# Self attentions of a two-layer latent stack: head halves on row halves, unrolled tiles, masks added by TensorE

## The chip, the cores and the metric

The kernel runs on one core of a Trainium2 chip. The metric is device time in microseconds for one execution. TensorE multiplies matrices from SBUF into PSUM, VectorE, ScalarE and GpSimd work elementwise and in reductions, and SyncE issues the DMAs; all run at once and wait for each other through semaphores. GpSimd doesn't read PSUM here; VectorE and ScalarE do.

## What is computed

A tensor `x` of 16 sequences with 64 tokens of 128 channels passes six residual blocks, each on a layer norm of `x`. Three of them hold a self attention with 16 heads of 8 channels:

```python
x = x + L0_cross_attention(ln(x), ctx)            # 1601 keys per sequence
x = x + L0_attn(ln(x))                            # stage one: causal self attention within a sequence
x = x + L0_experts(ln(x))                         # 8 experts, top 2
x = x + L1_block(ln(x), ctx)                      # cross attention, then self attention (stage two), then ffn
x = x + L1_attn(ln(x))                            # stage three: quantised, attends across the batch
x = x + L1_experts(ln(x))

def L0_attn(x):
    Q, K, V = heads(x @ W_Q), heads(x @ W_K), heads(x @ W_V)
    scores = einsum('bhqd,bhkd->bhqk', Q, K) / D_HEAD ** 0.5 + causal
    return merge(softmax(scores) @ V) @ W_o
```

Stage two has biases and no mask. Stage three has the tensor's first axis (16) as its length and its second (64) as its batch, so a token attends to 16 others; the kernel keeps groups of 64 tokens and masks out the pairs that don't belong together (`block_mask`). Everything is float32.

## The kernel before

The whole program is one pass over hand-written queues: each engine has its own list of instructions, and `at(engine, stage, step)` makes an engine wait for the semaphore of a named step. The stages `"a0"`, `"a1"` and `"a2"` are the self attentions one, two and three.

The 1024 tokens are 8 tiles (`PAIRS`) of 128, two groups of 64 tokens each. All heads of a group are done at once: the keys of a group are spread into a matrix of 128 rows (channels) by 16 x 64 columns (head, key), in which a column holds only the 8 channels of its head and zeros elsewhere. For a tile of two groups that is `kbd`, 128 x 2048. The steps of a tile, by line:

- `keys` (L436): VectorE copies the tile's queries to a buffer of its own (L439) and spreads the keys of the first group (L440, L390); GpSimd spreads those of the second (L398, L390) and waits for the copy of the queries. In its loop GpSimd runs a tiny instruction first (L257).
- `scores` (L327): TensorE multiplies queries by `kbd`, four calls of 128 rows x 64 columns with 512 moving columns; the two groups write to the two halves of the PSUM partitions.
- `subtract_max` (L442): VectorE adds the mask where there is one (L448), takes the maximum of each head (L450) and subtracts it (L451).
- ScalarE takes the exponential (L376) and copies the tile's values into a buffer with sum columns (L379).
- TensorE transposes the probabilities in 8 blocks (L344), ScalarE copies them out of PSUM (L384), TensorE multiplies them by the values (L352), 16 calls of 18 columns.
- `normalise` (L454): VectorE divides by the sums (L460, L464; in stage three one scaling more, L462).

Tiles alternate between two lanes, each with its own PSUM banks (scores in two, transposes and results in two more) and one buffer each for keys, probabilities and values. Each engine walks through rounds of two tiles; rounds 1 and 2 of four are in a loop (`Fori`). The keys of tile t + 2 go into the buffer of tile t, so they wait for the scores of t, and on VectorE they stand behind `subtract_max(t)`:

```python
for lane in range(2):
    subtract_max(i, lane)
    if not (isinstance(i, int) and i == ROUNDS - 1):
        keys(i + 1, lane)
    if lane == 1:
        normalise(i, 0)
    elif not (isinstance(i, int) and i == 0):
        normalise(i - 1, 1)
```

Before the first tile VectorE moves Q and K from PSUM (L406 to L416), writes the sum columns of both lanes (L433), spreads two tiles' keys and masks all values in one instruction (L483), which needs TensorE's value projection (L322) and frees its banks. After the last tile the heads are transposed (L314) and multiplied by the output weights. After its share of stages one and three, GpSimd splits the first experts' weights (L576, L578).

A call of a float32 matmul is two MATMUL instructions in the records; one with operands of type float32r is one instruction. TensorE calls go through a helper, so they show line 262.

## Time and profile before

| | us |
|---|---|
| median of 3 runs (1338.19 to 1339.38) | 1338.86 |
| the profiled execution | 1333.34 |
| its span | 1331.1 |

| engine | busy us | share of the span |
|---|---|---|
| TensorE matmul | 1041.1 | 78% |
| VectorE | 715.7 | 54% |
| ScalarE | 496.4 | 37% |
| GpSimd | 225.6 | 17% |

The mean granted TensorE clock is 0.883 of full speed. A row of the timeline gives start, duration, engine, line, operation, output tile and input tiles, the form (partitions x elements), a count when neighbours are merged (then the duration is from the first's start to the last's end), and in brackets the idle time before it with what ended it. PE is TensorE's matmul, DVE is VectorE, ACT is ScalarE, POOL is GpSimd. PEclk is the granted clock: 1.00 is 2.4 GHz, 0.50 is 1.2 GHz, a value between is a stretch with both. Tiles show under the name of the memory they lie in: `small` the queries of both lanes, `work_area` and `PT` the keys, `ctxT` Q, K and the result, `nat_area` the masked values, `PS` PSUM.

### The profile page before, as it was taken

How to read it: one execution, taken by the hardware profiler on the slowest of the kernel's cores; microseconds unless marked ns; L12 is line 12 of the kernel's file. 1: busy time of each engine (PE TensorE's matmuls, PEld its weight loads, DVE VectorE, ACT ScalarE, POOL GpSimd, SP SyncE). 2: the span in 40 equal slices, each digit the busy share in tenths (PEclk: the TensorE clock that was granted, in tenths of full speed). 3: DMA queues.
4: the chain of work that ended last, by engine and by line, in shares of the span. 5: the costliest groups of instructions: out<-in, count | busy, mean ns of one | idle time of the engine just before them, and what ended most of it. 6: DMA issues, size and time to landing. Idle time of an engine off the chain costs nothing.

```text
span 1331.1 us, 22303 instructions
## 1 busy us (share of the span) xinstructions
PE 1041.1 (78%) x9246; PEld 741.0 (56%) x9246; DVE 715.7 (54%) x1194; ACT 496.4 (37%) x649; POOL 225.6 (17%) x202
## 2 busy tenths in 40 slices
PE   3776765898873599999999999997575546739888
PEld 2455444787761266666666666665344333438767
DVE  3234775433343566666766666670585478763221
ACT  0235231222222156656656666655032202403333
POOL 2000460121213001111111111110161003400110
PEclk9898786999995689999999999999697767759999
DMA  8683000110201423323432332220001000000110
GB/s 270 202 347 131 1 0 1 31 41 24 97 0 50 151 104 129 106 103 114 148 122 104 122 113 104 103 76 18 1 1 32 1 0 0 1 0 16 33 47 16
DMA packets 41347, 98.48 MB, mean 74 GB/s; under 512 B 9976, under 2 KB 24960, under 8 KB 41264
## 3 DMA queue, kind: packets, MB, share of 16 engines
q1 hardware_dynamic: 41264, 97.29, 21.4%
q8 instruction: 63, 1.03, 0.3%
q14 instruction: 20, 0.16, 0.0%
HBM read 55.49 MB, written 0.73 MB: 42 GB/s over the span
## 4 chain that ended last, share of the span: by engine, by line
PE 50%; issue 16%; DVE 14%; ACT 7%; POOL 6%; SPq 3%; DMA 2%; POOLq 0%; DVEq 0%
PE PS L262 49%; DVE kl L1500 3%; ACT kh L1090 2%; ACT PT L1103 2%; DVE prT L1504 2%; POOL work_area L390 2%; SPq L905 2%; DVE mx L1515 2%; POOL PT L390 1%; DMA ctxT<-in_ctx_T 1%; DVE x L675 1%; POOL blank_g L257 1%; POOL rstd_all L281 1%; PE PS L292 1%; ACT work_area L654 1%
## 5 line engine op out<-in xcount | busy, mean ns | idle before, releaser
L1515 DVE TENSOR_REDUCE mx<-PS 128x2 f32<-128x1024 f32 x192 | 230.7, 1216 | 85.0 <-PE PS L262 84.9
L1103 ACT ACTIVATE PT<-PS 128x1024 f32<-128x1024 f32 (+1 forms) x208 | 212.3, 1021 | 94.7 <-PE PS L262 93.5
L262 PE MATMUL PS<-QB,QS 128*128 128x512 f32 x576 | 159.1, 425 | 23.9 <-DVE wcol L663 21.9
L262 PE MATMUL PS<-QB,KS 128*128 128x256 f32 (+1 forms) x832 | 166.2, 322 | 10.0 <-ACT PT L1103 9.5
L262 PEld LDWEIGHTS PS<-QB,QS 128*128 128x128 f32 x576 | 109.8, 201 | 61.0 <-issue 27.0
L262 PEld LDWEIGHTS PS<-QB,KS 128*128 128x128 f32 (+1 forms) x832 | 115.9, 186 | 43.8 <-issue 31.6
L262 PE MATMUL PS<-PT,work_area 128*32 128x128 f32 (+1 forms) x3328 | 134.4, 279 | 0.5 <-ACT PT L1103 0.5
L262 PE MATMUL PS<-KS,QB 64*128 64x512 f32 (+1 forms) x512 | 109.8, 458 | 13.1 <-DMA KS<-kl 9.5
L675 DVE SCALAR_TENSOR_TENSOR x<-PS,wcol,x 128x128 f32<-128x128 f32 x128 | 44.9, 351 | 138.2 <-PE PS L262 134.8
L262 PEld LDWEIGHTS PS<-PT,work_area 128*32 128x32 f32 (+1 forms) x3328 | 78.4, 109 | 46.3 <-issue 42.9
L262 PE MATMUL PS<-nat_area,work_area 128*128 128x128 f32 (+2 forms) x928 | 85.0, 275 | 13.7 <-DVE work_area L670 5.9
L262 PEld LDWEIGHTS PS<-nat_area,work_area 128*128 128x128 f32 (+2 forms) x928 | 81.8, 167 | 19.0 <-DVE work_area L670 7.6
L654 ACT ACTIVATE work_area<-PS 128x512 f32<-128x512 f32 x64 | 38.2, 598 | 126.7 <-PE PS L262 126.7
L292 PE MATMUL PS<-consts,u_all 128*128 128x128 f32 x64 | 15.7, 426 | 87.1 <-DVE u_all L275 66.5
L262 PE MATMUL PS<-ctxT,w_L_xattn_ck_w 128*128 128x512 f32 (+1 forms) x128 | 64.6, 588 | 22.4 <-DVE kl L1500 18.6
L262 PE MATMUL PS<-w_L_xattn_cv_w,ctxT 128*128 128x128 f32 (+1 forms) x416 | 78.7, 311 | 0.0
L262 PEld LDWEIGHTS PS<-KS,QB 64*128 64x128 f32 x512 | 45.9, 191 | 47.4 <-issue 16.0
L1090 ACT ACTIVATE kh<-PS,c_L_xattn_ck_b 128x512 fp32r<-128x512 f32 x64 | 38.1, 595 | 84.8 <-PE PS L262 69.4
L262 PEld LDWEIGHTS PS<-w_L_xattn_cv_w,ctxT 128*128 128x128 f32 (+1 forms) x416 | 55.8, 194 | 23.3 <-issue 22.8
L1500 DVE SCALAR_TENSOR_TENSOR kl<-PS,c_L_xattn_ck_b,kh 128x512 fp32r<-128x512 f32 x64 | 40.5, 632 | 49.1 <-ACT kh L1090 49.1
L987 POOL TENSOR_TENSOR QB<-QS,consts 128x1024 fp32r<-128x1024 f32 x16 | 31.2, 1954 | 200.8 <-PE PS L262 183.7
L576 POOL TENSOR_TENSOR QS<-nat_area,consts 128x512 fp32r<-128x512 f32 x24 | 25.9, 1081 | 220.8 <-DMA nat_area<-in_L_ffn_experts_w 124.7
(241 smaller groups left out, 1408.8 us busy)
## 6 DMA issues: line engine op xcount, KB each, us to landing
KS<-kh SPq DMA_DIRECT2D x32, 800.5 KB
ctxT<-in_ctx_T SPq DMA_DIRECT2D x24, 800.5 KB, 4.5
nat_area<-in_ctx_tiles SPq DMA_DIRECT2D x16, 832.0 KB, 6.8
KS<-kl SPq DMA_DIRECT2D x16, 800.5 KB
work_area<-in_ctx_T SPq DMA_DIRECT2D x8, 800.5 KB, 10.2
nat_area<-in_L_ffn_experts_w SPq DMA_DIRECT2D x24, 256.0 KB, 3.2
nat_area<-in_L_ffn_W SPq DMA_DIRECT2D x16, 256.0 KB, 3.0
KS<-mask_parts SPq DMA_DIRECT2D x32, 50.1 KB
```

The lines of the kernel that those rows point to most:

```text
L262: return T.matmul(o, l, r, start=start, stop=stop, **k)
L292: last = T.transpose(PS[:, 512 * (6 + h) + 128 * t:512 * (6 + h) + 128 * t + 128], src[:, 4 * h + t, :], ident)
L390: return eng.tensor_tensor(dst[:, 1024 * g:1024 * g + 1024].rearrange("p (h k) -> p h k", h=HEADS), src, hm, ALU.mult)
L654: ins = S.activation(g_act[:, c % 2, :], bank(2 * (c % 2)), ACT.Silu)
L675: last = V.scalar_tensor_tensor(x[:, 4 * t + q, :], PS[:, 512 * (4 + t) + q * 128:512 * (4 + t) + (q + 1) * 128], wcol[:, j, 4 * t + q:4 * ...
L905: sp.dma_start(dst, src).then_inc(loads, 16)
L987: P["qb_g"].done(G.tensor_tensor(QB[b % 3][:, :].rearrange("p (g h q) -> p g h q", g=4, h=4), QS[:, :, SEQ * b:SEQ * b + SEQ].unsqueeze(2) ...
L1090: P["keys_a"].done(S.activation(kh[:, c0:c0 + cw], bank(7, cw), ACT.Identity, bias=COLS["L1_xattn_ck_b"][:, 0:1]), f"kh{c}")
L1103: P["exp_a"].done(S.activation(PT[0:rows, par, :], PS[0:rows, 1024:2048], ACT.Exp), f"e{k}")
L1500: P["keys_v"].done(V.scalar_tensor_tensor(kl[:, c0:c0 + cw], bank(7, cw), COLS["L1_xattn_ck_b"][:, 0:1], kh[:, c0:c0 + cw], ALU.add, ALU.s ...
L1504: P["sum_v"].done(V.reciprocal(rsum, rsum), "sum")
L1515: ins = V.reduce_max(by_pair[:, :, j // 3, j % 3:j % 3 + 1], src, AX)
```

## The change

- Spread keys on row halves. Heads 0 to 7 live in channels 0 to 63, heads 8 to 15 in 64 to 127. Now the row half r holds only its own 8 heads: `SPREAD[t % 4]` is 128 x 1024 for a tile. The scores are four calls again, but each of 64 rows x 64 columns, with `tile_position=(64 * r, 64 * g)`: row half r writes to bank r, group g to its half of the partitions. The queries are read from `Q_all` directly.
- GpSimd alone spreads the keys, one instruction of 1024 elements per tile, into four buffers; it waits for the projected keys and from tile 4 on for the scores of tile t - 4. VectorE's copy of the queries and its half of the keys are gone, and GpSimd's tiny instruction too.
- The values are masked straight into a layout with room for the sum columns, `V_all[:, g, b, 0:18]`; ScalarE's copy of the values per tile is gone, and the sum columns are written once per stage, for all tiles.
- The masks are added by TensorE: before the scores, a matmul of the identity (`ident_r`) by the mask (`causal_r` or `block_r`, repeated over 8 heads) goes to each of the two score banks, 128 x 512, operands float32r, and the scores accumulate on it. VectorE's mask add is gone. `ident_r` and the masks are written twice by VectorE, 2 copies ahead of the layer norm of stage one and 2 copies ahead of `heads_vector` of stage three, since the memory (the first 256 columns of `small`) is used in between.
- All loops over tiles are unrolled. TensorE's order is weighted(t - 1), transposed(t), scores(t + 2); ScalarE's is copied(t - 1), exponential(t); VectorE's is subtract_max(t), normalise(t - 2). In stage three the keys' step has a semaphore value of its own, so GpSimd starts behind the quantised Q.

The core of the diff:

```diff
-        V_all = early[:, 512:512 + 2 * TOKENS]
+        V_all = early[:, 512:512 + 2 * PAIRS * 144].rearrange("p (g b c) -> p g b c", g=2 * PAIRS, b=8)
...
+        SPREAD = [a[:, 1024 * t:1024 * t + 1024] for a in (tail_area, PT[:, :, :].rearrange("p a n -> p (a n)")) for t in range(2)]
...
+            def scores(t):
+
+                L = LANE[t % 2]
+                at(T, st + "_g", f"kbd{t}")
+                if t >= 2:
+                    at(T, st + "_v", f"sub{t - 2}")
+                if mask is not None:
+                    T.wait_ge(mask_ready, 2 + int(st[1]))
+                    for r in range(2):
+                        mm(bank(L["bank"] + r), ident_r, mask.unsqueeze(1).broadcast_to([128, 8, SEQ]))
+                for r in range(2):
+                    rows = slice(64 * r, 64 * r + 64)
                     for g in range(2):
...
+                        o = 512 * (L["bank"] + r)
+                        last = mm(PS[SEQ * g:SEQ * g + SEQ, o:o + 512],
+                                  Q_all[rows, 128 * t + SEQ * g:128 * t + SEQ * g + SEQ],
+                                  SPREAD[t % 4][rows, 512 * g:512 * g + 512], start=mask is None,
+                                  skip_group_check=True, tile_position=(64 * r, 64 * g))
+                P[st + "_s"].done(last, f"s{t}")
...
+            scores(0)
+            scores(1)
+            for t in range(PAIRS):
+                if t >= 1:
+                    weighted(t - 1)
+                transposed(t)
+                if t + 2 < PAIRS:
+                    scores(t + 2)
+            weighted(PAIRS - 1)
...
+            for t in range(PAIRS):
+                if t >= 1:
+                    copied(t - 1)
+                pr = LANE[t % 2]["pr"]
+                at(S, st + "_v", f"sub{t}")
+                P[st + "_a"].done(S.activation(pr, pr, ACT.Exp, scale=scale), f"exp{t}")
+            copied(PAIRS - 1)
...
+            for t in range(PAIRS):
+                at(G, st + "_v", "k" if st == "a2" else f"k{t // 4}")
+                if t >= 4:
+                    at(G, st + "_s", f"s{t - 4}")
+                every = [128, 2, 8, SEQ]
+                P[st + "_g"].done(G.tensor_tensor(
+                    SPREAD[t % 4].rearrange("p (g h k) -> p g h k", g=2, h=8),
+                    K_all[:, 128 * t:128 * t + 128].rearrange("p (g k) -> p g k", g=2).unsqueeze(2).broadcast_to(every),
+                    consts[:, C_HM8:C_HM8 + 8].unsqueeze(1).unsqueeze(3).broadcast_to(every), ALU.mult), f"kbd{t}")
...
-                if mask is not None:
-                    link(V.tensor_tensor(p3, sc, mask.unsqueeze(1).broadcast_to([128, HEADS, SEQ]), ALU.add))
-                    sc = p3
...
+            for t in range(PAIRS):
+                subtract_max(t)
+                if t >= 2:
+                    normalise(t - 2)
+            for t in (PAIRS - 2, PAIRS - 1):
+                normalise(t)
...
+            V.tensor_copy(ident_r, ident).then_inc(mask_ready, 1)
+            V.tensor_copy(mask_ops[:, 128:256], consts[:, C_CAUSAL:C_CAUSAL + 128]).then_inc(mask_ready, 1)
             ln_all_vector(1, x, u_all)
...
-            link(quantise(X[:, 0, :], 3))
+            vdone(quantise(X[:, 0, :], 3), "a2_v", "k")
             link(V.tensor_tensor(unit[:, 0:1], qscale[:, 2:3], qscale[:, 3:4], ALU.mult))
...
+            V.tensor_copy(ident_r, ident).then_inc(mask_ready, 1)
+            V.tensor_copy(mask_ops[:, 128:256], consts[:, C_CAUSAL:C_CAUSAL + 128]).then_inc(mask_ready, 1)
+            heads_vector("a2", qscale[:, 2:3])
```

## Rows read from the trace of the kernel before

**Rows 1.** Windows over the three stages: start:end, length, busy us by engine, granted clock.

```profile
141.87:197.72 55.85, 39.77 (x384) 24.67 (x384) 42.10 (x52) 19.14 (x24) 29.37 (x20) 0.81 0.00 1
970.09:1014.96 44.87, 34.55 (x384) 21.80 (x384) 31.39 (x44) 20.41 (x25) 18.45 (x12) 0.89 0.00 1
1104.08:1166.75 62.67, 44.96 (x384) 26.55 (x384) 48.78 (x60) 23.71 (x27) 25.54 (x17) 0.72 0.00 1
```

**Rows 2.** Line L376 by stage: min/median/max ns, first and last start.

```profile
L376 ACT ACTIVATE work_area<-work_area x8: 1056/1057/1057, 149.2 to 191.0; 128x1024 f32<-128x1024 f32 x8
...
L376 ACT ACTIVATE work_area<-work_area x8: 1057/1057/1058, 975.6 to 1008.2; 128x1024 f32<-128x1024 f32 x8
...
L376 ACT ACTIVATE work_area<-work_area,unit x8: 1147/1148/1149, 1111.6 to 1159.7; 128x1024 f32<-128x1024 f32 x8
```

**Rows 3.** Timeline of VectorE, one tile of stage one: start us, us, what.

```profile
162.10 0.22 DVE L439 COPY small<-ctxT 128x128 f32 x1
162.49 1.23 DVE L390 TENSOR_TENSOR work_area<-ctxT,consts 128x1024 f32<-128x1024 f32 x1 [0.17 <-DVE small L439]
163.71 0.26 DVE L460 RECIPROCAL ssum<-PS 128x16 f32<-128x16 f32 x1
...
164.37 1.21 DVE L448 TENSOR_TENSOR work_area<-PS,consts 128x1024 f32<-128x1024 f32 x1
165.62 1.22 DVE L450 TENSOR_REDUCE smax<-work_area 128x16 f32<-128x1024 f32 x1
166.88 1.22 DVE L451 TENSOR_TENSOR work_area<-work_area,smax 128x1024 f32<-128x1024 f32 x1
```

**Rows 4.** Timeline of GpSimd, start of stage one.

```profile
136.64 1.90 POOL L390 TENSOR_TENSOR work_area<-ctxT,consts 128x1024 f32<-128x1024 f32 x1
```

**Rows 5.** Timeline of TensorE, stage two, and last transposes of stage one.

```profile
980.74 1.09 PE L262 MATMUL PS<-work_area,prT 128*64 128x18 f32 x32
981.76 1.09 PE L344 MATMUL PS<-consts,work_area 128*128 128x128 f32 x8
982.79 1.94 PE L262 MATMUL PS<-PT,small 128*64 128x512 f32 x8
984.56 1.07 PE L262 MATMUL PS<-work_area 128*64 128x18 f32 x32
...
988.19 1.94 PE L262 MATMUL PS<-work_area,small 128*64 128x512 f32 x8 [1.11 <-POOL work_area L390]
...
192.11 1.97 PE L344 MATMUL PS<-consts,work_area 128*128 128x128 f32 x8 [0.23 <-ACT work_area L376]
```

**Rows 6.** Timeline of ScalarE, stage two.

```profile
984.87 1.06 ACT L376 ACTIVATE work_area<-work_area 128x1024 f32<-128x1024 f32 x1 [0.96 <-DVE work_area L451]
...
987.11 1.02 ACT L384 ACTIVATE prT<-PS 128x1024 f32<-128x1024 f32 x1 [0.87 <-PE PS L344]
```

**Rows 7.** Windows over two stretches of the cross attention.

```profile
441.00:448.00 7.00, 5.14 (x14) 2.19 (x14) 5.54 (x5) 0.27 (x1) 0.00 (x0) 0.50 0.04 15
455.60:475.90 20.30, 19.43 (x80) 12.86 (x81) 13.91 (x16) 5.71 (x8) 0.00 (x0) 0.50 0.48 168
```

**Rows 8.** Timeline of TensorE: row-half maxima, and the first expert layer.

```profile
441.63 1.22 PE L262 MATMUL PS<-KS,QB 64*128 64x512 f32 x4 [9.50 <-DMA KS<-kl]
...
299.82 2.98 PE L262 MATMUL PS<-QB,QS 128*128 128x512 f32 x12
```

**Rows 9.** Timeline before the first scores of stage one.

```profile
134.13 3.71 PE L262 MATMUL PS<-w_L_attn_W_V,xT_all 128*64 128x128 f32 x64
...
139.54 2.28 DVE L483 TENSOR_TENSOR nat_area<-PS,consts 128x2048 f32<-128x2048 f32 x1
```

**Rows 10.** Timeline of VectorE, stage three.

```profile
1098.77 0.27 DVE L433 COPY work_area<-consts 128x32 f32<-128x32 f32 x2
...
1101.74 2.28 DVE L483 TENSOR_TENSOR nat_area<-PS,consts 128x2048 f32<-128x2048 f32 x1
...
1125.61 1.59 DVE L462 TENSOR_SCALAR ssum<-ssum,qscale 128x16 f32<-128x16 f32 x1
```

More of the change, by code:

```diff
@@ new lines, in transposed, with weighted @@
+            def transposed(t):
+                L = LANE[t % 2]
+                at(T, st + "_a", f"exp{t}")
+                if t >= 2:
+                    at(T, st + "_v", f"o{t - 2}")
+                for b in range(8):
+                    o = 512 * (L["bank"] + 2) + 128 * b
+                    last = T.transpose(PS[:, o:o + 128], L["pr"][:, 128 * b:128 * b + 128], ident)
+                P[st + "_t"].done(last, f"pT{t}")
+            def weighted(t):
+                L = LANE[t % 2]
+                at(T, st + "_a", f"pT{t}")
+                for b in range(8):
+                    for g in range(2):
+                        o = 512 * (L["bank"] + 2) + 18 * b
+                        last = mm(PS[SEQ * g:SEQ * g + SEQ, o:o + 18],
+                                  L["prT"][:, 128 * b + SEQ * g:128 * b + SEQ * g + SEQ], V_all[:, 2 * t + g, b, :])
+                P[st + "_o"].done(last, f"o{t}")
@@ L368, in heads_done @@
             else:
[L369 to L370 removed]
+                at(eng, st + "_v", f"o{PAIRS - 1}")
         def attn_scalar(st, scale=1.0):
[L373 to L384 removed]
@@ L400, in attn_vector, with copied @@
-        def attn_vector(st, q_bias, k_bias, v_bias, mask):
+            def copied(t):
+                at(S, st + "_t", f"pT{t}")
+                if t >= 2:
+                    at(S, st + "_o", f"o{t - 2}")
+                b = 512 * (LANE[t % 2]["bank"] + 2)
+                P[st + "_a"].done(S.activation(LANE[t % 2]["prT"], PS[:, b:b + 1024], ACT.Copy), f"pT{t}")
+            for t in range(PAIRS):
[4 more added lines that the diff above has]
+                P[st + "_a"].done(S.activation(pr, pr, ACT.Exp, scale=scale), f"exp{t}")
@@ L468, in two_tiles @@
-            def two_tiles(i):
-                for lane in range(2):
-                    subtract_max(i, lane)
-                    if not (isinstance(i, int) and i == ROUNDS - 1):
-                        keys(i + 1, lane)
-                    if lane == 1:
-                        normalise(i, 0)
-                    elif not (isinstance(i, int) and i == 0):
-                        normalise(i - 1, 1)
-            for lane in range(2):
-                keys(0, lane)
+                                    s2.unsqueeze(3).broadcast_to([128, 8, 2, HD]), ALU.mult), f"o{t}")
```

163 lines of the change are left out of this document (50 added, 113 removed).

## The prediction

> **What bounds the kernel now.** The change touches the three self attentions alone, so I read first the busy time in each of them, from the first score matmul to the end of the last normalise: 55.85, 44.87 and 62.67 us, with TensorE busy 71%, 77% and 72% and VectorE 75%, 70% and 78% [rows 1]. No engine is full. So each stage is a loop between engines, and its length is eight times a period. The exponentials of L376, one per tile of 128 tokens, give that period: first to last start is 41.8, 32.6 and 48.1 us over seven steps, so 5.97, 4.66 and 6.87 us per tile [rows 2].
>
> What sets it is seen in one tile of the first stage on VectorE: copy of q 0.22, half of the spread keys 1.23, the two normalise steps 0.66 from the first's start to the next operation's, mask add 1.21, maximum 1.22, subtraction 1.22 [rows 3]; with the gaps that is the whole period. GpSimd makes the other half of the keys in 1.90 [rows 4], and it can't begin before VectorE has copied q. TensorE then waits for GpSimd, 1.11 us before the scores at 988.19 [rows 5]. The chain runs in a circle: subtraction, q copy, keys, scores, next subtraction.
>
> **The change, part by part.**
>
> *VectorE* loses per tile the q copy, its key half, and in stages one and three the mask add. Left are 1.25 + 1.25 for maximum and subtraction (start to start) and 0.66 for the normalise steps: 3.2 us, and in the third stage one more small operation, L462, which the second stage's kind of step would put at 0.3 (by L460's 0.26). That is under the periods below, in the third stage by little.
>
> *GpSimd* spreads 1024 elements per tile as now, without VectorE beside it, so 1.90, into four buffers. It needs only the projected keys and, from tile 4 on, the scores of four tiles earlier. 1.90 is far under any period below, and the buffers let it run ahead: I cost it at nothing. Without that cover 1.90 would join the circle at each tile.
>
> *ScalarE* loses the value copy (0.40) and keeps exponential 1.06 and copy 1.02. From the exponential's start at 984.87 to the copy's at 987.11 are 2.24, with the transposes between them [rows 6]; the next exponential is queued behind the copy: 2.24 + 1.03 = **3.27 us per tile**, a floor for the loop.
>
> *TensorE, scores.* Now eight matmuls go as four pairs: 982.79 to 984.56, 1.77 us at full clock, 0.43 a pair [rows 5]. After the change each is 64x64, in its own quadrant. If all four quadrants run together there are two rounds: 0.86, plus up to 0.3 for entering and leaving that tiling. Do row halves overlap? The trace has one such place, the maxima of the cross attention: four row-half matmuls of 512 columns took 1.22 us at a granted clock of 0.50 [rows 7, 8], where 512 columns at 1.2 GHz are 0.43 and four in a row would be 1.71. So two at a time, with some overhead. I take 1.15 for the scores; the bounds are 0.86 and 2.0 (no overlap, with overhead).
>
> *TensorE, mask.* Two matmuls of 512 columns with fp32r operands are added per tile in stages one and three. Twelve of that kind, in the first expert layer, took 2.98 us, 0.25 each [rows 8], so 0.45 to 0.5 a tile. If they ran at the fp32 price (0.86 for 512 columns, two instructions at 0.43) it would be 1.7. I take 0.45, since those twelve have the same type and shape.
>
> *TensorE per tile*: transposes 1.03, mask 0.45, scores 1.15, weighted values 1.02 (pitches of [rows 5]) = 3.65. The order is w(t-1), T(t), mask and scores(t+2). The copy of tile t ends at c; mask and scores began at c - 1.12 and end at c + 0.48, the weighted values end at c + 1.48, the transposes and their copy add 2.15: **3.65 per tile** with the mask. Without it the scores end by c + 0.03 and ScalarE's 3.27 rules; I use 3.3.
>
> *Start of a stage.* The first scores wait for L483, which follows the value projection. In stage one the projection ends at 137.84 and L483 starts only at 139.54, behind the keys [rows 9]; now it starts at 137.9: 1.6 us earlier. I take the same 1.6 for stage two. Added before it: one copy for the sum columns (before, two), in the shadow of the projection; and two mask copies, 0.22 each by the q copy [rows 3], nothing beside them in stage one (+0.45). In stage three nothing hides them: GpSimd starts its keys at the same moment, and there L462, 16 elements wide, takes 1.59 while GpSimd spreads keys [rows 10], so it waited for it. Three copies behind one key operation each: up to 3 x 1.9 + 0.7, in place of the 2.97 us between L433 and L483 [rows 10]: +3.2 late (6.4 less 2.97, rounded down). Without such waits the three copies take 0.7 and L483 comes 2.3 early: the other bound.
>
> First scores at 1.2 GHz: 0.85 mask, 1.7 scores, 0.3 switching = 2.85 (2.0 without mask), then 2.5 on VectorE.
>
> *Sum*, before to after:
> Stage one: the first exponential starts 7.3 after the first scores (149.2 less 141.87), then 2.85 + 2.5 = 5.4; with 1.6 early and 0.45 late it comes 3.1 earlier. First to last exponential 41.8 to 6 x 3.65 + 3.3 + 2.5 = 27.7, where 2.5 is my allowance, an estimate, for tiles at the low clock. Last exponential to end 6.7 (197.72 less 191.0) to 2.24 + 1.03 for exponential, transposes and copy, 1.1 weighted values, 0.6 normalise = 5.0, if TensorE is still at 2.4 GHz. Gain 18.9.
> Stage two: 5.5 to 4.5 and 1.6 early, so 2.6 earlier; 32.6 to 7 x 3.3 + 2.5 = 25.6; tail 1.7. Gain 11.3.
> Stage three: 7.5 to 5.4 and 3.2 late, so 1.1 later; 48.1 to 25.3 + 2.5 + 1.5 for L462 behind GpSimd = 29.3; tail 1.8. Gain 19.5.
> The matmuls just behind each stage find a higher clock: 3 in all, an estimate. Together 53. The profiled execution is 1333.34 (span 1331.1), so 1280; it lies 5.5 under the median 1338.86, which gives **1286**. Nothing else depends on the stages but the first expert splits on GpSimd, which wait for its keys and come earlier.
>
> **A rule weighed.** L462's 1.59 us [rows 10] is one case; whether each of three copies in a row waits for a whole key operation no row shows. The Trainium skill, "SBUF — State Buffer", Terms, says that VectorE and GpSimd share a pair of SBUF ports under an exclusive lock, held for a full instruction, and that the loser blocks. It speaks against this placing of the mask copies. By it the start of stage three is 3.2 late, as in my sum; without it 2.3 early, and the result 5.5 lower. [...]
>
> **The rivals.**
> 1. Row halves don't overlap in fp32. Then scores are 2.0: +0.85, +0.8, +0.85 in six periods of the stages, and 1.7 in each start: 20 us more, **1306**. For it: no fp32 row half is in the trace. Against: the four row halves of [rows 8].
> 2. The mask matmuls cost the fp32 price: +1.2 in six periods of two stages and 2.5 in two starts: 19 more, **1305**.
> 3. The clock stays at 1.2 GHz through the stages. Per tile then 1.97 transposes (the last of [rows 5]), 0.86 mask, 2.0 scores, 2.0 weighted (twice 1.0) = 6.8, unmasked 6.0. First to last, six such and 4.2 without scores: 45, 40.2 and 45 against 41.8, 32.6 and 48.1, +7.7; starts -4.6 together: **1342**, about no change. For it: from 455.6 to 475.9 TensorE was 96% busy and the granted clock was 0.50 [rows 7]. Against: 0.89 over stage two, with TensorE 77% busy [rows 1].
> 4. Slower: the low clock and serial row halves together. 1.7 more in 18 periods and 5 in the starts, 36 on top of the third: **1378**. The mechanism is TensorE as the bound of each tile, and it decides from 5.83 us a tile, the present mean over 21 steps.
> 5. Better than my sum: no low-clock tiles after the first (7.5) and little blocking in stage three (4.7): **1274**.
> That the change does nothing is excluded: the removed operations lie on the circle.
>
> **How the numbers follow.** Forecast 57% (own range 1278 to 1296), rival one 14%, two 7%, three 7%, four 4%, five 11%. The range 1272 to 1316 leaves out most of three, all of four, and the tails of one and five: some 15 to 18 in 100. A measurement of this kernel tells about 0.2%, 2.7 us, from no change. Faster 0.91; within 0.2% 0.03 (part of rival three); slower 0.06 (four, and the upper end of three).
>
> **What would show it.** Starts of the exponentials 3.5 to 3.8 us apart in stages one and three, 3.2 to 3.4 in stage two. Score matmuls of a tile four at a time, the next kind starting about 1.1 us later; 2.0 means rival one. Mask matmuls 0.2 to 0.25 us apart; 0.43 or more and four of them means rival two. Granted clock above 0.9 over stages one and two; below 0.6 means rival three. GpSimd's keys done before tile 4 is exponentiated, and in stage three VectorE copies of about 2 us before L483. The forecast is wrong if VectorE, not TensorE or ScalarE, turns out busy without gaps, or if the unrolled instruction stream itself makes engines wait, which no row here shows.

## Result and the profile after

The changed kernel takes 1279.74 us in the median of 4 runs (1277.15 to 1284.19), the kernel before beside it 1338.53 (1334.08 to 1339.38): a ratio of 0.957, 95% interval 0.953 to 0.961, so 58.8 us faster. The profiled execution took 1281.95 us (span 1280.2), where the sum had said 1280.

Page of the kernel after, busy time of each engine and the chain that ended last:

```profile
PE 1022.1 (80%) x9278; PEld 731.4 (57%) x9278; DVE 657.4 (51%) x1131; ACT 483.0 (38%) x622; POOL 196.8 (15%) x178
...
PE 61%; DVE 16%; ACT 8%; issue 5%; SPq 4%; DMA 3%; POOL 3%; DVEq 0%; POOLq 0%; ACTq 0%
```

Exponentials of the kernel after by stage (now L402), first and last start, against [rows 2]; then windows from the first to the last of them, columns as in [rows 1]:

```profile
L402 ACT ACTIVATE work_area<-work_area x8: 1047/1048/1056, 149.0 to 175.0; 128x1024 f32<-128x1024 f32 x8
L402 ACT ACTIVATE work_area<-work_area x8: 1047/1048/1057, 957.5 to 982.9; 128x1024 f32<-128x1024 f32 x8
L402 ACT ACTIVATE work_area<-work_area,unit x8: 1139/1140/1148, 1084.7 to 1110.8; 128x1024 f32<-128x1024 f32 x8
...
148.96:175.02 26.06, 24.00 (x308) 15.52 (x308) 19.66 (x26) 13.79 (x14) 14.14 (x11) 0.93 0.01 2
957.46:982.91 25.45, 23.00 (x296) 15.00 (x296) 19.75 (x26) 13.80 (x15) 5.29 (x3) 0.87 0.01 2
1084.72:1110.82 26.10, 23.94 (x308) 16.02 (x308) 21.29 (x32) 14.44 (x15) 11.65 (x8) 0.93 0.01 1
```

First to last exponential went from 41.8, 32.6 and 48.1 us to 26.1, 25.4 and 26.1. TensorE is now busy 90 to 92% of these stretches, VectorE 75 to 82%. Below is one tile of stage one on TensorE, with ScalarE's copy beside it:

```profile
157.72 1.11 PE L264 MATMUL PS<-nat_area,work_area 128*64 128x18 f32 x32
158.77 1.09 PE L357 MATMUL PS<-consts,work_area 128*128 128x128 f32 x8
159.62 0.71 PE L264 MATMUL PS<-mask_ops 128*128 128x512 f32 x2
159.90 1.02 ACT L395 ACTIVATE prT<-PS 128x1024 f32<-128x1024 f32 x1 [1.58 <-PE PS L357]
160.26 1.09 PE L264 MATMUL PS<-work_area,ctxT 64*64 64x512 f32 x8
161.28 1.11 PE L264 MATMUL PS<-nat_area,prT 128*64 128x18 f32 x32
```

From start to start the weighted values take 1.05, the transposes 0.85, the mask 0.64 and the scores 1.02: 3.55 us, without a gap. ScalarE idles 1.58 in it, before its copy. In the single records the eight instructions of the scores come as two rounds of four, 0.48 apart, and the two of the mask start 0.32 apart. The exponentials follow each other in 3.55 us in stages one and three and in 3.25 in stage two, once the first two or three steps are over.

### The profile page after: what moved, and what is told of

Read it like the earlier page. It is cut to its first block, busy times and chain, and to the rows that moved or that the text cites. A ratio compares the mean times of both kernels' runs of the same rounds, so it can differ in the third digit from the quotient of the medians.

```text
span 1280.2 us, 22033 instructions
## 1 busy us (share of the span) xinstructions
PE 1022.1 (80%) x9278; PEld 731.4 (57%) x9278; DVE 657.4 (51%) x1131; ACT 483.0 (38%) x622; POOL 196.8 (15%) x178
## 4 chain that ended last, share of the span: by engine, by line
PE 61%; DVE 16%; ACT 8%; issue 5%; SPq 4%; DMA 3%; POOL 3%; DVEq 0%; POOLq 0%; ACTq 0%
PE PS L264 57%; DVE kl L1493 3%; ACT kh L1081 3%; ACT PT L1094 3%; DVE prT L1497 2%; SPq L896 2%; PE PS L357 2%; DVE mx L1508 2%; DMA ctxT<-in_ctx_T 1%; PE PS L294 1%; POOL rstd_all L283 1%; DVE x L667 1%; DVE u_all L277 1%; DMA work_area<-in_ctx_T 1%; DVE stats_all L269 1%
## 5 line engine op out<-in xcount | busy, mean ns | idle before, releaser
L264 PE MATMUL PS<-nat_area,work_area 128*128 128x128 f32 (+2 forms) x1312 | 100.8, 261 | 17.2 <-DVE work_area L662 5.9
L264 PEld LDWEIGHTS PS<-nat_area,work_area 128*64 128x64 f32 (+1 forms) x1312 | 96.3, 165 | 31.3 <-ACT work_area L395 12.3
L264 PEld LDWEIGHTS PS<-w_L_xattn_cv_w,ctxT 128*128 128x128 f32 (+1 forms) x416 | 55.8, 194 | 23.3 <-issue 22.8
L294 PEld LDWEIGHTS PS<-consts,u_all 128*128 128x128 f32 x64 | 12.5, 223 | 88.5 <-DVE u_all L277 41.0
L978 POOL TENSOR_TENSOR QB<-QS,consts 128x1024 fp32r<-128x1024 f32 x16 | 31.2, 1955 | 202.1 <-PE PS L264 186.0
## 6 DMA issues: line engine op xcount, KB each, us to landing
work_area<-in_ctx_T SPq DMA_DIRECT2D x8, 800.5 KB, 10.2
```

What stands on the lines that cost most here:

```text
L264: return T.matmul(o, l, r, start=start, stop=stop, **k)
L294: last = T.transpose(PS[:, 512 * (6 + h) + 128 * t:512 * (6 + h) + 128 * t + 128], src[:, 4 * h + t, :], ident)
L978: P["qb_g"].done(G.tensor_tensor(QB[b % 3][:, :].rearrange("p (g h q) -> p g h q", g=4, h=4), QS[:, :, SEQ * b:SEQ * b + SEQ].unsqueeze(2) ...
```

## The experiments

Of each run the table has what the verdicts rest on: first to last exponential by stage, and the steady step in the masked stages (stages one and three; two values where they differ) and in stage two, all in us, from the profiled execution. The steady step is that of the last tiles. The runs without masks, doubled, without the second all-reduce, with stage two's wait filled, and the last one are single runs, and one run's total says little about 3 us: the changed kernel's own runs spread from 1277.15 to 1284.19. Much of this spread arises before stage one: the last addition to `x` of the first cross attention starts anywhere from 119.23 to 126.02 us in the fourteen profiles, though all kernels have the same instructions up to there. So the stages' own times tell more than the totals.

| kernel | one | two | three | step, masked | step, two |
|---|---|---|---|---|---|
| after | 26.1 | 25.4 | 26.1 | 3.55 | 3.25 |
| after, once more | 24.5 | 25.4 | 26.1 | 3.55 | 3.25 |
| no masks | 25.5 | 25.5 | 25.6 | 3.25 | 3.25 |
| doubled | 27.2 | 28.5 | 27.3 | 4.01 | 3.94 |
| masks on VectorE | 31.2 | 25.5 | 33.3 | 4.13, 4.41 | 3.25 |
| full rows | 28.7 | 27.5 | 28.7 | 4.25 | 3.78 |
| stage two's wait filled | 26.1 | 22.7 | 26.1 | 3.55 | 3.25 |
| first scores first | 24.5 | 26.5 | 26.1 | 3.55 | 3.25 |
| no second all-reduce | 24.5 | 24.1 | 24.6 | 3.55 | 3.25 |
| ScalarE helps, one tile | 24.5 | 26.4 | 27.3 | 3.55 | 3.25 |
| ScalarE helps, two tiles | 24.5 | 26.5 | 24.6 | 3.55 | 3.25 |
| waits filled in all stages | 24.5 | 22.7 | 24.6 | 3.55 | 3.25 |
| the same without masks | 22.7 | 22.7 | 24.0 | 3.25 | 3.25 |

**Is TensorE the bound? Its work doubled in places.**

```diff
-                    for r in range(2):
+                    for r in (0, 1, 0, 1):
                         mm(bank(L["bank"] + r), ident_r, mask.unsqueeze(1).broadcast_to([128, 8, SEQ]))
-                for r in range(2):
+                for r in (0, 1) if mask is not None else (0, 1, 0, 1):
                     rows = slice(64 * r, 64 * r + 64)
```

> The work of TensorE is doubled in one place, the output stays right: the two mask matmuls of a tile are issued twice in stages one and three, and the four score calls twice in stage two. Theory (TensorE-bound): masked tiles go from 3.55 to 4.2 apart (two more at 0.32), and in stage two, where TensorE has 1.03 + 1.02 + 1.05 = 3.10 of work within 3.25, the second scores cost 1.0 less the slack of 0.15, so 4.1 apart; span longer by 16 to 18 us. Rival (TensorE has slack behind VectorE or ScalarE): under 0.3 more per masked tile and under 0.5 in stage two.

Measured: 1292.5 us. Stage one's TensorE in the doubled kernel:

```profile
165.95 1.09 PE L357 MATMUL PS<-consts,work_area 128*128 128x128 f32 x8
166.79 1.17 PE L264 MATMUL PS<-mask_ops 128*128 128x512 f32 x4
167.90 1.09 PE L264 MATMUL PS<-PT,ctxT 64*64 64x512 f32 x8
```

With two more mask matmuls the scores start 1.11 after the first mask matmul, where it was 0.64, and all of the difference came through to the step (3.55 to 4.01, 0.46 more); in stage two the second scores cost 0.69 (3.94). TensorE is the bound of the masked tiles. Both steps are shorter than the 4.2 and 4.1 that I had expected, and the span grew by 10.5 us and not by 16 to 18. The further pair costs 0.23 each, near the 0.25 of [rows 8], where I had taken 0.32. The first pair costs no more: its two start 0.32 apart, but it stretches the way from transposes to scores only from 1.02 (stage two) to 0.85 + 0.64 = 1.49, by 0.47.

**The row halves alone, undone.**

```diff
-                                  Q_all[rows, 128 * t + SEQ * g:128 * t + SEQ * g + SEQ],
-                                  SPREAD[t % 4][rows, 512 * g:512 * g + 512], start=mask is None,
-                                  skip_group_check=True, tile_position=(64 * r, 64 * g))
+                                  Q_all[:, 128 * t + SEQ * g:128 * t + SEQ * g + SEQ],
+                                  SPREAD[t % 4][:, 512 * g:512 * g + 512], start=mask is None,
+                                  skip_group_check=True)
```

> The score calls use all 128 rows in place of 64 (same calls, same columns, no tile positions on rows), so heads h and h + 8 are summed into each other and the output isn't the reference's; the time is that of scores without row halves. Theory: the four calls take 1.75 in place of 1.02, so masked tiles are 4.25 to 4.3 apart, unmasked ones 3.8 (3.10 of TensorE plus 0.75, less nothing), and the first two scores of each stage, at 1.2 GHz, cost 1.7 more each: 5.1 + 3.9 + 5.1 and 3 times 2 to 3.4, so 20 to 24 us more. Rival (row halves save only switching, or the loop is bound elsewhere): under 0.3 per tile, under 8 us.

Measured: 1290.3 in the median of 4, ratio to before 0.965 (0.962 to 0.969), 10.6 us over the changed kernel. TensorE in stage one with full rows:

```profile
167.46 1.94 PE L264 MATMUL PS<-work_area,ctxT 128*64 128x512 f32 x8
169.23 1.06 PE L264 MATMUL PS<-nat_area,work_area 128*64 128x18 f32 x32
```

The scores take 1.77 in place of 1.02, and the steps are the expected ones (4.25; 3.78). But the whole is half of the 20 to 24 expected (by the spans of the two profiled executions it is 16.1, 2.6 of it before the mask copies of stage one). The stages' first to last grew only by 2.6 (4.2 against the second profile of the changed kernel), 2.0 and 2.6. In the masked stages all steps from the second on are 4.25 here, and in stage two the longest is 4.69, while the changed kernel has steps of 4.77 and 5.64 there. So part of what the row halves take from TensorE comes back in the first tiles. That such a long step is the low clock's is shown below, where a wait is filled.

**The masks, on VectorE again.**

```diff
-                if mask is not None:
-                    T.wait_ge(mask_ready, 2 + int(st[1]))
-                    for r in range(2):
-                        mm(bank(L["bank"] + r), ident_r, mask.unsqueeze(1).broadcast_to([128, 8, SEQ]))
...
+                    link(V.tensor_tensor(p3, sc, m.unsqueeze(1).broadcast_to([128, HEADS, SEQ]), ALU.add))
+                    sc = p3
                 link(V.reduce_max(L["smax"], sc, AX))
```

> The masks go back to VectorE (one addition of 1024 elements per tile), the mask matmuls are gone, all else as in the changed kernel; the output stays right. Theory: VectorE then has 3.75 for three operations and 0.66 for the normalise steps, so it is the bound with 4.4 us per tile in stages one and three, against 3.55; seven steps give 6 us more in each, the start about 0.4 to 0.6, the end nothing: 13 us, ratio to the kernel before about 0.966. Rival (the circle through ScalarE and TensorE has room for the addition, since scores run two tiles ahead): 3.55 stays, no difference.

Measured: 1295.6 in the median of 4, ratio to before 0.969 (0.965 to 0.973), 15.8 over the changed kernel. VectorE in stage one:

```profile
169.96 1.21 DVE L453 TENSOR_TENSOR work_area<-PS,consts 128x1024 f32<-128x1024 f32 x1
171.21 1.22 DVE L455 TENSOR_REDUCE smax<-work_area 128x16 f32<-128x1024 f32 x1
172.46 1.23 DVE L456 TENSOR_TENSOR work_area<-work_area,smax 128x1024 f32<-128x1024 f32 x1
173.61 0.25 DVE L465 RECIPROCAL ssum<-PS 128x16 f32<-128x16 f32 x1
...
174.10 1.21 DVE L453 TENSOR_TENSOR work_area<-PS,consts 128x1024 f32<-128x1024 f32 x1
```

VectorE works without a gap, 4.14 a tile, so it would be the bound: 15.8 of the 58.8 us hang on the masks' new place. (The rows show 3.65 for the three operations and about 0.5 for the normalise steps, a little under my 3.75 and 0.66.) The steady step comes only in the last two steps of stage one. In the tiles before, the subtraction takes 1.43 to 2.27 in place of 1.22, while GpSimd splits the experts' weights:

```profile
158.37 2.27 DVE L456 TENSOR_TENSOR work_area<-work_area,smax 128x1024 f32<-128x1024 f32 x1
```

Masks and row halves are the only parts that were taken back one at a time. How the rest of the 58.8 us divides among the keys on GpSimd alone, the queries read in place, the values' layout and the unrolled order, no run shows.

**What the masks cost where they are now.**

```diff
-            attn_tensor("a0", 1, *(W["L0_attn_W_" + n][:, :] for n in "QKVo"), mask=causal_r)
+            attn_tensor("a0", 1, *(W["L0_attn_W_" + n][:, :] for n in "QKVo"))
...
-            heads_tensor("a2", X[:, 2, :], ident, block_r)
+            heads_tensor("a2", X[:, 2, :], ident)
```

> The mask matmuls of stages one and three are left out, so the scores there are unmasked; everything else is as in the changed kernel. Theory (TensorE is the bound of the masked tiles, 3.55 us apart, and ScalarE's circle of exponential, transposes and copy that of the unmasked ones, 3.25): starts of the exponentials go from 3.55 to 3.25 apart in stages one and three, their first-to-last from 26.0 and 26.1 to about 23.8, the first scores end 0.9 to 1.2 earlier, together 6 us off the span. Rival (VectorE, 3.2 us of work per tile and gaps, is the bound): 3.55 stays, and only the 2 us of the two starts go.

Measured: 1282.5 in a single run, where 6 us less than 1279.7 was expected. The steady step did fall to 3.25. But the stages are about as long as with masks (25.5, 25.5 and 25.6), and the start of stage one tells why (two operations of TensorE, then windows):

```profile
152.43 1.90 PE L264 MATMUL PS<-nat_area,prT 128*64 128x18 f32 x32
154.26 1.97 PE L357 MATMUL PS<-consts,work_area 128*128 128x128 f32 x8
...
151.00:154.00 3.00, 3.00 (x38) 1.57 (x32) 1.42 (x2) 1.71 (x2) 1.34 (x1) 0.50 0.03 5
154.00:157.00 3.00, 3.00 (x20) 2.09 (x21) 1.49 (x3) 0.73 (x1) 0.56 (x1) 0.50 0.00 0
```

TensorE runs at 1.2 GHz for two windows here; the steps are 5.53 and 3.79 where the masked kernel has 4.77 and 3.55, or none above 3.56 in its second profile. Ahead of the low clock TensorE had waited: 2.39 before its first scores and 2.96 before the first transposes. The next run tests whether these waits are the cause.

**A wait filled, in stage two alone.**

```diff
             scores(0)
             scores(1)
+            if st == "a1":
+                T.wait_ge(mask_ready, 4)
+                for _ in range(8):
+                    mm(bank(2), ident_r, causal_r.unsqueeze(1).broadcast_to([128, 8, SEQ]))
```

> Changed kernel, with eight more matmuls of TensorE in stage two alone, of the kind of the mask's (fp32r, 512 columns, about 0.23 each at 2.4 GHz), into a bank that the next transposes overwrite; they stand between the second scores and the first transposes, where TensorE idles 2.9 us (the two mask copies of stage three are moved ahead of stage two for it). Theory: the low clock of the third tile of stage two (granted 0.50 from 959 to 962, exponentials 5.64 and 3.64 apart) comes from that idle time; filled, the clock stays at 1.00 and the steps are 3.2 to 3.3 from the second on: first to last exponential 25.4 to 22.8, 2.6 us off the span. Rival: the clock goes by something else (the long busy or idle time before); 5.6 stays somewhere in the first four steps and nothing is gained.

Measured: 1275.4. Stage two in the second profile of the changed kernel, windows over the first tiles, then the windows of the filled one:

```profile
956.00:959.00 3.00, 2.03 (x16) 1.17 (x16) 2.18 (x2) 1.81 (x2) 1.33 (x1) 0.83 0.00 0
959.00:962.00 3.00, 3.00 (x41) 2.05 (x34) 1.92 (x2) 1.07 (x2) 1.84 (x1) 0.50 0.00 0
962.00:965.00 3.00, 3.00 (x16) 1.62 (x15) 0.98 (x3) 1.25 (x2) 0.06 (x1) 0.53 0.03 5
```

```profile
954.00:957.00 3.00, 2.13 (x17) 1.46 (x19) 2.97 (x3) 1.10 (x2) 2.20 (x2) 1.00 0.00 0
957.00:960.00 3.00, 2.91 (x48) 1.92 (x44) 2.03 (x3) 1.93 (x2) 1.88 (x1) 1.00 0.00 0
```

The clock stays at 2.4 GHz, the steps are 3.16 and then six of 3.25, and the stage takes 22.7 where it took 25.4; stages one and three, not touched, stayed at 26.1. Eight idle matmuls of 2.1 us in all, done while TensorE waited, shortened the stage by 2.8 us. This is one profile, but chance is unlikely: in each of the ten profiles in which this wait isn't filled, one step of stage two is 0.9 to 2.4 us over the steady one, and in none of the three in which it is filled. That the two mask copies were moved ahead of stage two isn't the reason either: the version with two tiles on ScalarE, below, has them there too, and its step of 5.65.

**The first scores ahead of the masked values.**

```diff
             scores(0)
+            at(T, st + "_v", "V")
+            T.wait_ge(sum_columns, int(st[1]) + 1)
             scores(1)
```

> The wait of TensorE for the masked values is moved from before the first tile's scores to before the second's (the first tile's banks are free). In the changed kernel the first maximum starts 4.2 us after the value masking starts in stage one (142.15 to 146.38): 2.28 for the masking, then mask and scores at 1.2 GHz. Theory: now the first scores run beside the masking, the first maximum starts 2.9 after the masking's start in stage one, 2.3 in stage two (VectorE itself), and nothing in stage three, whose first scores wait for GpSimd's keys; 1.3 + 1.9 + 0, about 3 us off the span, ratio to the changed kernel 0.9975. Rival (the second tile sets the pace, since its scores still wait for the masking): under 1 us.

> The changed kernel itself, unchanged, beside the two versions: 1277 to 1284, and the same rows within 0.3 us.

Measured, side by side: 1277.1 (ratio to before 0.957, 0.954 to 0.959) against 1279.7 for the changed kernel (0.957, 0.955 to 0.960). The difference of 2.6 is about what was expected, but the intervals overlap, so it isn't shown. In stage one the first maximum starts 2.3 after the masking's start (139.65 against 137.32, where it was 4.2). In stage two it does so too (3.6 to 2.3), but the second exponential follows after 4.04 in place of 3.16, and most of the gain is lost there. The transposes before it, at 948.45, run at 1.2 GHz after a wait of 2.52 (1.97 us, where they took 1.09).

**GpSimd's late start in stage three.** GpSimd, VectorE and the first mask matmul in the changed kernel:

```profile
1069.01 0.90 POOL L955 PARTITION_ALL_REDUCE gmax<-amax  x1 [7.29 <-DVE amax L1427]
...
1073.85 0.16 DVE L1579 TENSOR_TENSOR unit<-qscale 128x1 f32<-128x1 f32 x1
...
1074.32 0.29 DVE L445 COPY nat_area<-consts 128x256 f32<-128x256 f32 x1
1074.53 2.28 DVE L474 TENSOR_TENSOR nat_area<-PS,consts 128x2048 f32<-128x2048 f32 x1
1076.81 3.76 POOL L411 TENSOR_TENSOR work_area<-ctxT,consts 128x1024 f32<-128x1024 f32 x2 [6.89 <-DVE nat_area L474]
1078.95 1.19 PE L264 MATMUL PS<-mask_ops 128*128 128x512 f32 x2 [8.56 <-POOL work_area L411]
```

The keys could start at 1073.8, with the quantised Q. They start at 1076.81, so VectorE's copies ran unhindered and the first scores waited for GpSimd instead.

```diff
-            all_max(3, "Q", "qx_v")
+            at(G, "qx_v", "Q")
+            P["q_all"].done(G.tensor_copy(gmax[:, 3:4], amax[:, 3:4]), "Q")
```

> In stage three the second all-reduce of GpSimd (the maximum of Q over the partitions) is replaced by a copy of the partition's own maximum, so Q is quantised with a scale per partition and the output isn't the reference's. In the changed kernel GpSimd's first keys start 2.96 us after the key step (1076.81 against 1073.85), just as VectorE's masking of the values ends. Theory A: an elementwise operation of GpSimd starts no sooner than about 7.8 us after the start of an all-reduce (1069.01 to 1076.81; before the change 1093.74 to 1101.73); without it the keys start within 0.3 us of the key step, and then the small VectorE copies behind it either take their 0.22 to 0.29 (no lock) or about 1.9 each (the lock of my forecast, 3 to 5 us in all). Theory B: VectorE's operations hold GpSimd back until the masking of the values ends; then the keys still start 2.9 to 3.0 us after the key step.

Measured: 1276.1 in a single run. GpSimd and VectorE without the second all-reduce:

```profile
1062.69 0.19 POOL L1005 COPY gmax<-amax 128x1 f32<-128x1 f32 x1 [7.26 <-DVE amax L1428]
...
1067.55 0.16 DVE L1580 TENSOR_TENSOR unit<-qscale 128x1 f32<-128x1 f32 x1
...
1068.22 2.29 DVE L474 TENSOR_TENSOR nat_area<-PS,consts 128x2048 f32<-128x2048 f32 x1
1069.77 3.76 POOL L411 TENSOR_TENSOR work_area<-ctxT,consts 128x1024 f32<-128x1024 f32 x2 [6.89 <-issue]
```

Both theories fall. The keys start while the value masking still runs, so B is out. They also start 2.2 us after the key step and not at once, so A is out as I put it: what comes 6.89 before them is the end of a plain copy, not of an all-reduce. The instruction records have a MODIFY_POOL_CONFIG of GpSimd at that point, at 1062.90 here and at 1069.86 in the changed kernel, and in all fourteen profiles 6.87 to 7.18 us pass from the end of the last operation before it to the first elementwise one (7.09 in the kernel before). The reading that fits all of them, though no run took the change of code away: GpSimd changes its loaded code between the all-reduces and the elementwise operations, and the copy still ran under the first. The Trainium skill, "GPSIMD Engine Reference", Instruction dispatch, gives the first call to a freshly loaded kernel about 6 us behind such an instruction; the traces agree in kind and show 6.9 to 7.2. Whether the value masking or VectorE's copies would be hindered by keys that start at once stays open: no run had them start so early.

**Idle engines before stage three's first scores.**

```diff
+            for h in range(8):
+                ins = S.activation(SPREAD[0].rearrange("p (g h k) -> p g h k", g=2, h=8)[:, :, h, :],
+                                   K_all[:, 0:128].rearrange("p (g k) -> p g k", g=2), ACT.Copy,
+                                   scale=consts[:, C_HM8 + h:C_HM8 + h + 1])
...
+            for h in range(2):
+                ins = S.activation(V_all[:, :, :, 8 * h:8 * h + 8],
...
+                                   ACT.Copy, scale=consts[:, C_HEAD + h:C_HEAD + h + 1])
```

> As the one before, and in stage three idle engines take the work ahead of the first scores: ScalarE spreads the first tile's keys (8 activations) while VectorE quantises Q, and masks the values (2 activations); mask copies and sum columns are written earlier, where VectorE waits for TensorE. Theory: the first scores of stage three then start within 0.3 of the key step in place of 5.1 us after it (1078.95 against 1073.85); the second scores wait for the values masked by ScalarE or for GpSimd's second keys, which costs up to 1 again: 4 to 5 us less than the one before, 7 to 8 in all, ratio to the changed kernel 0.994. Rival (GpSimd's keys, late behind the all-reduce, hold the second scores back): first exponential only 1 to 2 us earlier.

Measured: 1270.6 in the median of 5, ratio to before 0.953 (0.950 to 0.955), 9.1 under the changed kernel. The first scores start 0.1 after the key step and the first exponential 4.4 after it, where it was 10.9 (1084.72 less 1073.85). The second scores waited for GpSimd:

```profile
1065.33 1.89 POOL L420 TENSOR_TENSOR work_area<-ctxT,consts 128x1024 f32<-128x1024 f32 x1 [6.94 <-issue]
...
1067.48 0.90 PE L264 MATMUL PS<-mask_ops 128*128 128x512 f32 x2 [3.35 <-POOL work_area L420]
```

and the second exponential came 6.10 after the first. So ScalarE took the second tile's keys too, and VectorE the values again:

```diff
+            for t in range(2):
+                for h in range(8):
...
-            for t in range(st == "a2", PAIRS):
+            for t in range(2 * (st == "a2"), PAIRS):
```

> As the version in which ScalarE helps, but ScalarE spreads the keys of the first two tiles of stage three (16 activations, 0.31 each) and VectorE masks the values itself, behind the key step. Theory: GpSimd's first keys can't come before 6.9 us after the end of its all-reduce, and in the version before the second tile's scores waited for them (exponentials 6.10 apart). Now the second scores start about 2.5 after the key step in place of 5.1, the first two exponentials are 2.5 to 3.3 apart and stage three's last exponential comes 2 to 3 us earlier: 1268 where that one had 1270.6. Rival: the first tile's keys done later or tiles at the low clock give the gain back: 1270 to 1272.

Measured: 1266.9 in the median of 5, ratio 0.949 (0.946 to 0.951); the interval overlaps a little with that of the version before (0.950 to 0.955). The stage itself shows the gain: the last exponential of stage three starts 29.6 us after the key step; before this edit it was 31.7, in the changed kernel 37.0.

**All waits filled.**

```diff
+        def warm(n, k, late=2):
+            T.wait_ge(mask_ready, late)
+            for _ in range(n):
+                mm(bank(k), ident_r, causal_r.unsqueeze(1).broadcast_to([128, 8, SEQ]))
...
+            if st == "a2":
+                warm(8, 0, late)
             scores(0)
...
             scores(1)
+            warm(6, 2, late)
...
                 if t + 2 < PAIRS:
                     scores(t + 2)
+                else:
+                    warm(4, 0, late)
```

> As the version with two tiles on ScalarE, and TensorE's waits at the start and the end of the three stages are filled with idle matmuls of the mask's kind (6 before the first transposes of a stage, 8 before the first scores of stage three, 4 in place of each of the last two scores, 5 and 4 around the transposes of the heads), into banks that nobody reads before they are overwritten. Theory: the tiles at the low clock at the start (2.5 us in stages two and three) and the last tile's 1.9 to 2.0 at 1.2 GHz for weighted values, transposes of the heads and output projection (3.8) fall to half: 2.6 + 2.6 at the starts, 1 + 1 + 1.9 behind stages one and two, 1 in stage three, up to 12 us in all, 1257. Rival: the fillings delay the matmuls behind them where they run at the low clock themselves (0.43 each), and the clock doesn't hold: within 3 us of the version without.

Measured: 1259.3 in the median of 6, ratio to before 0.942 (0.939 to 0.945), 20.4 us under the changed kernel and 7.6 under the version without filling. The end of stage two on TensorE, in the changed kernel and then filled:

```profile
987.66 1.90 PE L264 MATMUL PS<-nat_area,work_area 128*64 128x18 f32 x32 [1.11 <-ACT work_area L395]
991.50 1.97 PE L316 MATMUL PS<-consts,ctxT 128*128 128x128 f32 x8 [1.95 <-DVE ctxT L438]
993.40 3.79 PE L264 MATMUL PS<-w_L_xattn_so_w,ctxT 128*128 128x128 f32 x16
```

```profile
974.24 1.11 PE L264 MATMUL PS<-nat_area,work_area 128*64 128x18 f32 x32 [0.18 <-ACT work_area L413]
975.28 1.43 PE L264 MATMUL PS<-mask_ops 128*128 128x512 f32 x5
977.29 1.09 PE L321 MATMUL PS<-consts,ctxT 128*128 128x128 f32 x8 [0.59 <-DVE ctxT L459]
...
979.16 1.95 PE L264 MATMUL PS<-w_L_xattn_so_w,ctxT 128*128 128x128 f32 x16
```

From the last exponential of stage two to the end of the output projection it is 14.3 us in the changed kernel, 14.1 in the version without filling and 10.3 filled, a gain of 3.8. In stage one the last two figures are 9.9 and 9.5, where the fillings themselves delay the transposes by half a microsecond, and in stage three, up to the maximum behind the last tile, 6.2 and 5.5. Stage two's exponentials gained 3.8 (26.5 to 22.7), the others nothing, since no tile of theirs ran at the low clock without filling. 3.8 + 3.8 + 0.4 + 0.8 is 8.8 of the 10.6 us between the two spans (1269.3 and 1258.7). I had expected 12: stage three's start held nothing more to win, and stage one's end little.

**The masks' price with the clock held.** The filled version, with the mask matmuls left out by the edit shown above.

> The filled version without the mask matmuls of stages one and three (their scores are unmasked, so the output isn't the reference's); the idle matmuls at the starts and ends stay. In the changed kernel, leaving the masks out brought nothing, since one more tile of each stage ran at 1.2 GHz (steps 5.53 and 3.79, then 3.25). Theory: that loss came from the waits at the start of the stage, so with the waits filled all steps are 3.25, first to last exponential 22.7 in all three stages (24.46, 22.66 and 24.56 in the filled version), 3.6 us off the span beside 0.9 for the masks ahead of the first tiles. Rival: without the mask's work TensorE is too idle in every tile to keep the clock, and a step over 5 comes back in stages one and three.

Measured: 1256.1 in a single run, which lies inside the range of the filled version (1254.7 to 1263.9), so the total shows no price. The steps do: they are 3.25 in stage one from the second on, 22.7 in all against 24.5, so the loss of the run without masks came from what TensorE did at the start of the stages. Which part of that, isn't separated for stage one: this version has the waits filled, but the first scores ahead of the masked values too. In stage three one step is 4.20 and the stage 24.0. There VectorE stands behind GpSimd:

```profile
1068.27 1.03 POOL L593 TENSOR_TENSOR QS<-nat_area,consts 128x512 fp32r<-128x512 f32 x1
...
1069.37 1.27 POOL L595 TENSOR_TENSOR QS<-nat_area,QS 128x512 fp32r<-128x512 f32 x1
1069.39 1.29 DVE L492 TENSOR_SCALAR ssum<-ssum,qscale 128x16 f32<-128x16 f32 x1
```

L492, 16 elements wide, takes 0.23 later in this stage and 1.29 here; it ends 0.04 after GpSimd's operation. That is the waiting of [rows 10], now by the expert splits.

## Why the prediction was right

- **What bounds it.** With the parts of the circle of [rows 2 to 5] gone, the stages shrank about as the sum had it. From the layer norm ahead of a stage to the transposes of the heads, stage one gained 19.4 us (predicted 18.9) and stage two 10.2 (11.3). Stage three gained 25.1 from its first quantising to its end (19.5).
- **Per tile, masked.** 3.55 for 3.65, TensorE-bound, as the doubled and the full-row kernels show. The mask is 0.47 (0.45 taken), the weighted values 1.05 (1.02) and the transposes 1.02 (1.03, in stage two); the tenth of a microsecond is the scores', 1.02 for 1.15: entering and leaving the quadrants cost less than I allowed.
- **Per tile, unmasked.** 3.25 for 3.3. ScalarE idles 1.28 of it, all for the transposes, and TensorE has about 0.15 left; that points to the circle exponential, transposes, copy as the bound. The same step stands in both kernels without masks, but no run changed ScalarE's part, so this is argued and not shown.
- **Rivals one and two** (no overlap of row halves, the mask at the fp32 price) are out by the tile above: its scores come in rounds of four 0.48 apart, and its mask in two instructions that lengthen the tile by 0.47.
- **Rivals three and four** (low clock throughout) are out: the granted clock is 0.93, 0.87 and 0.93 of full speed from the first to the last exponential. In stage two that is below the 0.9 that I had named as a sign.
- **Low-clock allowance of 2.5 a stage.** It was right in size for stage two alone: the first-to-last figures are 26.1, 25.4 and 26.1 where 7 steady steps would be 24.9, 22.8 and 24.9, so 1.2, 2.6 and 1.2 over them. It isn't a constant either: the second profile of the same kernel has 24.5 in stage one.
- **Start of stages one and two.** L474 starts with the end of the value projection, as said (142.15). From the first matmul of the scores or mask to the first exponential it is 4.5 in stage one and 3.7 in stage two, where I had 5.4 and 4.5: the granted clock is 1.00 from the value projection on (138 to 148 us in stage one), and I had priced the first scores at 1.2 GHz. That gain was given back by the low clock two tiles later.
- **Start of stage three: the step that failed.** I had three small VectorE copies waiting for a key operation of GpSimd each, 3.2 us late. They took 0.23, 0.22 and 0.29. GpSimd was not there yet: its first keys came 6.9 us after its all-reduce. In its place came the wait of the first scores for late keys, and the start came out 0.4 earlier than before the change (5.1 from L1579 to the first mask matmul, where 5.5 lay between the same step and the first scores). Up to the first exponential it is 10.9 for 13.0, so 2.1 earlier, where the sum had it 1.1 later. What looks like the lock is there all the same: the copy L445 takes 1.36 in stage one, where GpSimd's keys run from 138.41, and 0.29 in stage three, where they don't yet.

```profile
139.10 1.36 DVE L445 COPY nat_area<-consts 128x256 f32<-128x256 f32 x1
```

The late start of GpSimd was in the trace before. I had read that stretch only from VectorE's side:

```profile
1093.74 0.89 POOL L964 PARTITION_ALL_REDUCE gmax<-amax  x1 [7.09 <-DVE amax L1436]
...
1101.73 0.18 POOL L257 TENSOR_TENSOR blank_g<-consts 128x1 f32<-128x1 f32 x1 [7.09 <-issue]
```

- **The 1.5 us for L462 behind GpSimd.** The same operation (now L467) took 0.23 to 0.53 in the tiles, 0.4 over its usual time in all, so the allowance was about 1 too much; the step was TensorE's, and VectorE had room for it.
- **3 us from a higher clock behind the stages: they didn't come.** The last tile's weighted values (1.90), the transposes of the heads (1.97) and most of the output projection still ran at 1.2 GHz, since TensorE waits for ScalarE's copy twice at the end (1.11 each). The filled version shows what they would be (1.11, 1.09 and 1.95 in stage two). From the last exponential to the end of the last normalise step stage one took 5.9 us, 5.0 predicted.
- **The total.** The parts of 54.7 us stand beside a span shorter by 50.9; 2.5 of the difference were lost before the mask copies of stage one already, in code that the change doesn't touch (its last addition starts at 123.43 in place of 120.90, inside the spread given above); the copies themselves delayed the layer norm by 0.28. Another 2.2 were lost between stages one and two, and 1.1 came back behind stage three; why, no run shows. Stage three gained 5.6 more than predicted, while 1.1 of stage two and the 3 us behind the stages didn't come, and 3.8 were lost outside the parts: that this nearly cancelled in the total is luck. My 5.5 us between the profiled execution and the median went the wrong way: the profiled one here was 2.2 over its median, and 1286 lies 6 above the measured 1279.74 for that reason.

## What to carry to other kernels

When you move an operation to an engine that has gaps, or take one away, look at what the gaps do: matmuls in a wait of TensorE held its clock at 2.4 GHz here, and taking work away can bring less than its own time: without masks stage one went from 26.1 or 24.5 us to 25.5, and with the waits filled from 24.5 to 22.7. A wait of TensorE at the start or end of a stage that can't be removed may be filled with matmuls into a bank that is overwritten next. And when an engine starts late with "issue" as the reason, find out what it did before it: the order of its kinds of work may be the cause.

## What the runs showed of the hardware

- Four quadrants of 64x64 run together with fp32 operands: 512 columns in 0.48 to 0.54 a round. The eight instructions of a tile's scores take 1.02 in this form, and 1.77 with 128 rows.
- Identity times mask with fp32r operands costs 0.23 us for each 512 columns where four stand in a row. Two alone, between fp32 transposes and quadrant matmuls, start 0.32 apart and lengthen the way by 0.47.
- GpSimd starts its first elementwise operation 6.87 to 7.18 us after the last all-reduce ahead of stage three, and after a copy that takes the all-reduce's place too (6.89).
- ScalarE spreads one tile's keys in 8 activations of 128 elements, 0.31 each, 2.45 in all, where GpSimd takes 1.90 in one.
- The same kernel can have tiles at the low clock at the start of a stage in one profile and none in the next: 26.1 and 24.5 us from the first to the last exponential of stage one.
